# Three graph layers' edge loops: sums ahead of weights, features ahead of scaling, four product buffers

## The chip, the cores and the metric

The kernel runs on one core of a Trainium2 chip. Times are device microseconds of one execution. Engine names in the profile: PE is TensorE (PEld its weight loads), DVE is VectorE, ACT is ScalarE, POOL is GpSimd, SP is SyncE.

## The reference

The input is a graph of 6250 nodes (160 numbers each: 64 scalars and 32 vectors of three) and 100000 edges. Four layers run one after the other, each followed by a residual and a layer norm. The change is in layers 1 to 3. Each of them does this for every edge (layer 3 is shown; layer 1 has relu and no `e0`, layer 2 has no cross product and also counts edges):

```python
hid = silu(edge_scalars @ fc_w1 * _inv(R))
w = hid @ fc_w2 * _inv(FC_HID)
w1, w2, w3, w4, w5 = split(w, [64, 128, 160, 192], axis=-1)
es = h_s[edge_src];  ev = h_v[edge_src]
m_s1 = w1 * es * e0
m_s2 = w4 * einsum('eci,ei->ec', ev, e1) * _inv(3)
m_v1 = (w2 * es)[:, :, None] * e1[:, None, :]
m_v2 = w3[:, :, None] * ev * e0[:, :, None]
m_v3 = w5[:, :, None] * cross(ev, e1[:, None, :]) * _inv(2)
agg = segment_sum(concatenate(m_s1, m_s2, m_v1, m_v2, m_v3), edge_dst)
```

## The kernel before

Layer 0 has an edge loop of its own. Layers 1 to 3 share one function, `edge_loop(L)`, which the change edits. Edges lie sorted by destination block of 128 nodes. A step takes 256 edges (two groups `g` of 128) that all belong to one block, and each layer has 440 steps, four to an iteration of a hardware loop (`u` is 0 to 3). Below, step k is the k-th of the 440.

In each step of a layer the engines do this, joined by semaphores alone:

- SyncE loads the edges' records (`rec`, L840) and features (`efr`, L841) into one of four slots, after product k-4 is done.
- GpSimd gathers 2 times 128 node rows (L911) from HBM into `gatx`, after the record has landed.
- TensorE turns the features (`transposed`, L975), makes the hidden layer (`hidden`, L979) and the weights (`weights`, L985, 448 columns, into one of two banks `pW`), and adds up the products of one block with a one-hot matrix (`sums`, L993, twice 480 columns, 385 in layer 2, into one of two banks `pS`).
- ScalarE copies the turned features out of PSUM (`features`, L924), applies the activation (`activated`, L929), multiplies part of the weights by `e0` in place (`scaled`, L935, not in layer 1), and writes six blocks of the product (`axes`, L945, six instructions).
- VectorE makes the rest of the product (`product`, L1041 to L1070, in layer 2 to L1067) in one of two halves of `tp`, makes the one-hot matrix (L1056), and in the middle of it adds a finished sum to the block's row in SBUF (`keep`, L1081).

The order within an engine's step is written out by hand. TensorE's step k is: weights of step k+2, first half of the sums of k, transpose of k+3, second half of the sums of k, hidden layer of k+3. ScalarE's step k is: axes of k, scaling of k+1, features of k+2, activation of k+2. VectorE's product k has the keep of k-2 in it.

The waits that matter: `weights(k+2)` waits for the activation of k+2 and for product k (it frees the bank `pW`). `sums(k)` waits for product k, axes k and the keep of k-2 (bank `pS`). `hidden(k+3)` waits for the copy of the features of k+3. `features(k+2)` waits for the transpose of k+2. The product k waits for its gather, for `summed` of k-2 (half of `tp`) and for `w_done` of k, which is the scaling in layers 2 and 3 and the weights themselves in layer 1.

Of the kernel before, what the change touches and what calls it, by code (L numbers as in the profile page):

```python
# [12 lines left out]
G = 2  # L13
# [7 lines left out]
RH, TPW = 10, 544  # L21
# [43 lines left out]
def build(nc, ins, out, N, E, CH):  # L65
    fp32, i32 = mybir.dt.float32, mybir.dt.int32
    ALU, ACT, AX = mybir.AluOpType, mybir.ActivationFunctionType, mybir.AxisListType
# [6 lines left out]
    with ctx:  # L74
# [26 lines left out]
        def mark(name, total):  # L101
            if name not in known:
                known[name] = Mark(sem(name))
            known[name].base += known[name].total
            known[name].total = total
            return known[name]
# [48 lines left out]
        gat = sb("gat", [P, 4, G, F])  # L155
# [688 lines left out]
        def edge_loop(L):  # L844
# [13 lines left out]
            tp_ready = sig4("tp_ready", 1, NP)  # L858
            summed = sig4("summed", 1, NP)
            kept = sig4("kept", 1, NP)  # L860
            zeroed = mark("sums_zeroed", 2 + (L.n == 2))
            TW, VS = L.width, L.vs
            fc1, fc2 = W[f"fc1_{L.n}"], W[f"fc2_{L.n}"]
            EW = G * L.efw
            pE, pH, ramp = BK[0][:, 0:128], BK[0][:, 128:256], BK[1][:, 0:P]
            pW, pS = [BK[2], BK[3]], [BK[4], BK[5]]
            w_done = w_ready if L.y0 is None else w_scaled
            NM = 3 if L.cross else 1

            def w_of(u):  # L870
                return pW[u % 2][:, 0:448].rearrange("p (g f) -> p g f", g=G)

            def after(i, u, k):
                return (i, u + k) if u + k < 4 else (i + 1, u + k - 4)

            def last(u, k):
                return u + k < 4

            with nc.Block() as block:
# [19 lines left out]
                @block.gpsimd  # L899
                def _(po):  # L900
                    if L.n == 2:
                        nc.gpsimd.memset(tp[:, :, :, 64 + 384:64 + 385], 1.0).then_inc(zeroed.h, 1)

                    def gather(i, u):
                        po.wait_ge(rec_in[u].h, rec_in[u].at(i * 32 + 32))
                        po.sem_inc(pool_tick, 1)

                        po.wait_ge(tp_ready.h, tp_ready.free(i, u, 4))
                        po.sem_inc(pool_tick, 1)
                        for g in range(G):  # L910
                            nc.gpsimd.indirect_dma_start(  # L911
                                out=gatx[:, u, g, 0:L.row], out_offset=None, in_=tables[L.n][:, :],
                                in_offset=IOff(ap=rec[:, u, g, L.idx:L.idx + 1].bitcast(i32), axis=0))\
                                .then_inc(gat_in[u].h, 16)

                    with po.Fori(0, QP) as i:
                        for u in range(4):
                            gather(i, u)

                @block.scalar  # L920
                def _(ac):
                    def features(i, u):
                        ac.wait_ge(ef_t.h, ef_t.done(i, u))
                        nc.scalar.activation(efT[0:EW, u % 2, :], pE[0:EW, :], ACT.Copy).then_inc(ef_ready.h, 1)  # L924

                    def activated(i, u):
                        ac.wait_ge(hid.h, hid.done(i, u))
                        func, by = {1: (ACT.Relu, 1.0), 2: (ACT.Silu, 0.25), 3: (ACT.Silu, 0.125)}[L.n]
                        nc.scalar.activation(hT[:, u % 2, :], pH, func, scale=by).then_inc(hid_ready.h, 1)  # L929

                    def scaled(i, u):
                        ac.wait_ge(w_ready.h, w_ready.done(i, u))
                        for g in range(G):
                            c = slice(224 * g + 64, 224 * g + 160)
                            done = nc.scalar.activation(pW[u % 2][:, c], pW[u % 2][:, c], ACT.Copy,  # L935
                                                        scale=rec[:, u % 4, g, L.y0:L.y0 + 1])
                        done.then_inc(w_scaled.h, 1)

                    def axes(i, u):
                        ac.wait_ge(sv_ready.h, sv_ready.done(i, u))  # L940
                        t = tp[:, u % 2]
                        for g in range(G):
                            for k in range(3):
                                lo = 64 + 96 + VS * k
                                done = nc.scalar.activation(t[:, g, lo:lo + 64], t[:, g, 0:64], ACT.Copy,  # L945
                                                            scale=rec[:, u, g, L.y + k:L.y + k + 1])
                        done.then_inc(axes_done.h, 1)

                    def step(i, u, end=False):
                        axes(i, u)  # L950
                        if L.y0 is not None and (not end or last(u, 1)):
                            scaled(*after(i, u, 1))
                        if not end or last(u, 2):
                            features(*after(i, u, 2))
                            activated(*after(i, u, 2))

                    for u in range(2):
                        features(0, u)
                        activated(0, u)
                    if L.y0 is not None:  # L960
                        scaled(0, 0)
                    with ac.Fori(0, QP - 1) as i:
                        for u in range(4):
                            step(i, u)
                    for u in range(4):
                        step(QP - 1, u, True)

                @block.tensor
                def _(pe):
# [18 lines left out]
                    def sums(i, u, g):  # L988
                        if g == 0:
                            pe.wait_ge(tp_ready.h, tp_ready.done(i, u))  # L990
                            pe.wait_ge(axes_done.h, axes_done.done(i, u))
                            pe.wait_ge(kept.h, kept.free(i, u))
                        done = nc.tensor.matmul(pS[u % 2][:, 0:TW], oh[:, u, g, :], tp[:, u % 2, g, 64:64 + TW],  # L993
                                                start=g == 0, stop=g == G - 1)
                        if g == G - 1:
                            done.then_inc(summed.h, 1)

                    def step(i, u, end=False):
                        if not end or last(u, 2):
                            weights(*after(i, u, 2))  # L1000
                        sums(i, u, 0)
                        if not end or last(u, 3):
                            transposed(*after(i, u, 3))
                        sums(i, u, 1)
                        if not end or last(u, 3):
                            hidden(*after(i, u, 3))
# [13 lines left out]
                def _(ve):  # L1020
# [6 lines left out]
                        return bass.AP(tensor=a.tensor, offset=a.offset, ap=[a.ap[0]] + dims)  # L1027

                    def product(i, u, ahead):
                        t, w, row = tp[:, u % 2], w_of(u), gatx[:, u]  # L1030
                        tv = t[:, :, 160:160 + 3 * VS].rearrange("p g (i f) -> p g i f", i=3)
                        v = row[:, :, 64:160].rearrange("p g (k c) -> p g k c", k=3)

# [1 line left out]
                            return w[:, :, lo:lo + 32].unsqueeze(2).to_broadcast([P, G, 3, 32])  # L1035
                        ve.wait_ge(rec_in[u].h, rec_in[u].at(i * 32 + 32))
                        ve.wait_ge(gat_in[u].h, gat_in[u].at(i * 32 + 32))
                        ve.wait_ge(summed.h, summed.free(i, u))
                        ve.wait_ge(w_done.h, w_done.done(i, u))

                        nc.vector.tensor_tensor(t[:, :, 0:128].rearrange("p g (j c) -> p g j c", j=2),  # L1041
# [31 lines left out]
                    def block_of(i, u):  # L1073
                        return ve.value_load(L.blocks[0:1, bass.ds(i * 4 + u, 1)], min_val=0, max_val=NB - 1)

                    def keep(i, u, b):
                        ve.wait_ge(summed.h, summed.done(i, u))
                        row = acc[:, bass.ds(b, 1), :].rearrange("p o f -> p (o f)")

                        ve.wait_ge(kept.h, kept.free(i, u, 1))  # L1080
                        nc.vector.tensor_tensor(row, row, pS[u % 2][:, 0:TW], ALU.add).then_inc(kept.h, 1)  # L1081

                    ve.wait_ge(zeroed.h, zeroed.at(2 + (L.n == 2)))
                    for u in range(2):
                        product(0, u, None).then_inc(tp_ready.h, 1)
                    for u in range(2, 4):
                        product(0, u, (0, u - 2, block_of(0, u - 2))).then_inc(tp_ready.h, 1)
                    with ve.Fori(1, QP) as i:
                        for u in range(4):
                            back = (i - 1, u + 2) if u < 2 else (i, u - 2)  # L1090
                            product(i, u, (*back, block_of(*back))).then_inc(tp_ready.h, 1)
                    for u in range(2, 4):
                        keep(QP - 1, u, block_of(QP - 1, u))
                    ve.wait_ge(kept.h, kept.done(QP - 1, 3))

# [1045 lines left out]
```

## Time and profile before

| | us |
|---|---|
| median of 3 runs | 10883.89 (10879.81 to 10886.22) |
| the profiled execution's own time | 10889.87 |
| its span, first to last instruction | 10887.1 |
| edge loop of layer 1: first product to last | 5756.5 to 7258.5 |
| edge loop of layer 2 | 7567.9 to 9017.4 |
| edge loop of layer 3 | 9195.7 to 10698.6 |

Over the whole span TensorE is busy 81%, VectorE 80%, ScalarE 64% and GpSimd 59%. These shares are means over layer 0, three edge loops and the passes over nodes between them. The clock column of the windows is the granted TensorE clock as a share of full speed. In the timeline, a line's first number is the start in us from the span's start and the second the duration. "x2" merges two instructions, and brackets give the idle time before the instruction and what ended it.

### The profile page before, as it was taken

The page shows a single profiled execution, that of the slowest core. Times are in us where ns is not written, and L with a number is a line of the kernel's source. Part 1 is how long each engine was busy: PE and PEld are TensorE (multiplying, and loading weights), DVE is VectorE, ACT ScalarE, POOL GpSimd, SP SyncE. Part 2 cuts the span into 40 slices and gives each one's busy share as a digit, 9 for nine tenths or more (in the row PEclk, how much of TensorE's full clock was granted, in tenths as well). Part 3 has the DMA queues.
Part 4 walks back from the last instruction along what each step waited for, and adds up shares of the span by engine and source line. Part 5 has one row for each costly group of instructions (what it writes and reads, how often), then busy time and mean ns, then how long its engine had stood idle before and what let it go on. Part 6 is the DMA issues. An engine that isn't in the chain of part 4 may idle for free. (4 is left out here: it accounts for less than half of the span.)

```text
span 10887.1 us, 242413 instructions
## 1 busy us (share of the span) xinstructions
PE 8864.7 (81%) x46500; PEld 6212.8 (57%) x46501; DVE 8658.5 (80%) x31135; ACT 6961.3 (64%) x26255; POOL 6465.1 (59%) x9502
## 2 busy tenths in 40 slices
PE   3570069999999999999997888887888887888887
PEld 1250058888888888888884444445444445444445
DVE  6850069999999999999978999974666666999995
ACT  0020058888888888888875666644777775777774
POOL 0577777777777777777525555531555551555551
PEclk9965589999999999999999999985999998999996
DMA  7433322222222212221123444441333333444443
GB/s 292 44 82 73 71 42 37 36 37 36 37 36 37 36 35 37 36 36 34 20 43 84 90 89 89 89 67 36 58 58 58 58 57 66 90 90 90 90 89 58
DMA packets 1798441, 691.91 MB, mean 64 GB/s; under 512 B 1586190, under 2 KB 1677258, under 8 KB 1798346
## 3 DMA queue, kind: packets, MB, share of 16 engines
q0 software_dynamic: 219136, 411.56, 15.6%
q1 hardware_dynamic: 1572154, 275.26, 15.1%
q10 hardware_dynamic: 7056, 4.02, 0.1%
q8 instruction: 36, 0.59, 0.0%
q14 instruction: 59, 0.48, 0.0%
HBM read 514.24 MB, written 171.77 MB: 63 GB/s over the span
## 5 line engine op out<-in xcount | busy, mean ns | idle before, releaser
L911 POOL DMA_INDIRECT shared<-table,rec x2640 | 2564.6, 971 | 2236.0 <-DMA efr<-rec_dst 786.9
L993 PE MATMUL bank<-tp,oh 128*128 128x480 f32 (+1 forms) x5280 | 2352.4, 541 | 7.2 <-DVE tp L1070 4.2
L945 ACT ACTIVATE tp<-tp,rec 128x64 f32<-128x64 f32 x7920 | 2031.2, 335 | 239.3 <-DVE tp L1041 174.8
L985 PE MATMUL bank<-w_fc,hT 128*128 128x448 f32 x2640 | 1346.2, 592 | 589.2 <-ACT hT L929 573.0
L993 PEld LDWEIGHTS bank<-tp,oh 128*128 128x128 f32 x5280 | 902.0, 191 | 831.9 <-issue 819.4
L782 POOL DMA_INDIRECT rec_dst<-ACC x784 | 811.6, 1035 | 529.7 <-issue 497.3
L1041 DVE TENSOR_TENSOR tp<-bank,shared 128x256 f32<-128x256 f32 x1320 | 560.6, 425 | 653.9 <-PE bank L993 516.6
L1630 ACT ACTIVATE shared<-bank 128x512 f32<-128x512 f32 x1760 | 942.9, 586 | 122.1 <-PE bank L1705 119.3
L1594 POOL DMA_INDIRECT gat<-table,rec x880 | 889.5, 1011 | 220.5 <-issue 202.6
L929 ACT ACTIVATE hT<-bank 128x128 f32<-128x128 f32 x1320 | 366.5, 278 | 989.2 <-PE bank L979 964.3
L1581 POOL DMA_INDIRECT rec_src<-ACC x784 | 841.6, 1074 | 208.0 <-issue 185.4
L1705 PE MATMUL bank<-ident,tp 128*128 128x128 f32 x7040 | 933.2, 276 | 3.0 <-ACT tp L813 2.0
L985 PEld LDWEIGHTS bank<-w_fc,hT 128*128 128x128 f32 x2640 | 394.3, 188 | 835.6 <-DVE tp L1070 549.0
L979 PEld LDWEIGHTS bank<-efT,w_fc 128*128 128x128 f32 (+1 forms) x2640 | 457.7, 187 | 689.8 <-ACT efT L924 613.0
L1705 PEld LDWEIGHTS bank<-ident,tp 128*128 128x128 f32 x7040 | 830.6, 147 | 3.8 <-ACT tp L813 2.3
L1081 DVE TENSOR_TENSOR ACC<-ACC,bank 128x480 f32 (+1 forms) x1320 | 813.8, 616 | 4.2 <-PE bank L993 4.1
L1048 DVE TENSOR_TENSOR shared<-shared,rec 128x288 f32<-128x288 f32 x1760 | 722.4, 452 | 0.0
L1714 PE MATMUL bank<-w_vvlin,shared 128*128 128x32 f32 x5280 | 711.3, 272 | 0.0
L1659 ACT ACTIVATE shared<-shared,a 128x128 f32<-128x128 f32 x1760 | 562.4, 390 | 212.9 <-DVE a L1946 212.9
L1728 PEld LDWEIGHTS bank<-w_val,shared 128*128 128x128 f32 x5280 | 681.3, 192 | 0.0
L813 ACT ACTIVATE tp<-t_sv,rec 128x64 f32<-128x64 f32 x2640 | 674.1, 342 | 3.5 <-DVE t_sv L1845 3.5
L813 ACT ACTIVATE tp<-vsv,rec 128x64 f32<-128x64 f32 x2640 | 674.6, 339 | 0.0
(249 smaller groups left out, 21496.4 us busy)
## 6 DMA issues: line engine op xcount, KB each, us to landing
shared<-table,rec POOLq DMA_INDIRECT x2640
rec_dst<-tp SPq DMA_DIRECT2D x44, 900.0 KB, 23.6
ACC<-in_attrs SPq DMA_DIRECT2D x56, 623.0 KB, 5.1
rec_src<-tp SPq DMA_DIRECT2D x44, 730.0 KB, 19.8
efr<-rec_src SPq DMA_DIRECT2D x440, 64.0 KB
efr<-rec_dst SPq DMA_DIRECT2D x440, 64.0 KB
ACC<-in_attrs SPq DMA_DIRECT2D x196, 130.0 KB
rec<-rec_dst SPq DMA_DIRECT2D x1320, 10.0 KB
```

The source lines that it names most:

```text
L782: nc.gpsimd.indirect_dma_start(out=rec_dst[:, :], out_offset=IOff(ap=stage_i[:, u, c, 0:1], axis=0), in_=stage[:, u, c, 1:RD + 1], in_offs ...
L813: last = nc.scalar.activation(t[:, g, lo:lo + 64], s[:, g, :], ACT.Copy, scale=rec[:, u % 4, g, L.y + k:L.y + k + 1])
L911: nc.gpsimd.indirect_dma_start(out=gatx[:, u, g, 0:L.row], out_offset=None, in_=tables[L.n][:, :], in_offset=IOff(ap=rec[:, u, g, L.idx:L. ...
L945: done = nc.scalar.activation(t[:, g, lo:lo + 64], t[:, g, 0:64], ACT.Copy, scale=rec[:, u, g, L.y + k:L.y + k + 1])
L985: nc.tensor.matmul(pW[u % 2][:, 0:448], hT[:, u % 2, :], fc2[:, :], start=True, stop=True)\
L993: done = nc.tensor.matmul(pS[u % 2][:, 0:TW], oh[:, u, g, :], tp[:, u % 2, g, 64:64 + TW], start=g == 0, stop=g == G - 1)
L1048: done = nc.vector.tensor_tensor(vy[:, g], ranges(row[:, g, 64:65], [[32, 3], [32, 3], [1, 32]]), ranges(rec[:, u, g, L.y:L.y + 1], [[2, 3 ...
L1081: nc.vector.tensor_tensor(row, row, pS[u % 2][:, 0:TW], ALU.add).then_inc(kept.h, 1)
L1581: nc.gpsimd.indirect_dma_start(out=rec_src[:, :], out_offset=IOff(ap=srow_i[:, h, c, RS:RS + 1], axis=0), in_=srow[:, h, c, 0:RS], in_offs ...
L1594: nc.gpsimd.indirect_dma_start(out=gat[:, s4, g, :], out_offset=None, in_=tables[0][:, :], in_offset=IOff(ap=rec[:, s4, g, 1:2].bitcast(i3 ...
L1630: nc.scalar.activation(into[:, g, :], pT[g][:, :], ACT.Copy).then_inc(copied_.h, 1)
L1705: last = nc.tensor.transpose(pT[g][:, 128 * k:128 * k + 128], tp[:, slot, g, lo:lo + 128], ident[:, :])
```

## The change

In the edge loops of layers 1 to 3 the first half of the sums of step k is issued before the weights of k+2. ScalarE copies the features of k+2 before it scales the weights of k+1. There are four product buffers instead of two (the halves of `tp`, and two in the tiles `gat` and `shared`, which are free in these loops), and four sum banks instead of two. The keep in product k is now that of k-3. In layer 2 the constant column of ones is set in four buffers instead of two.

```diff
-            zeroed = mark("sums_zeroed", 2 + (L.n == 2))
+            zeroed = mark("sums_zeroed", 2 + 4 * (L.n == 2))
+            products = [tp[:, 0], tp[:, 1], gat.rearrange("p u g f -> p (u g f)")[:, 0:G * TPW].rearrange(
+                "p (g f) -> p g f", g=G), shared[:, 3136:3136 + G * TPW].rearrange("p (g f) -> p g f", g=G)]
-            pW, pS = [BK[2], BK[3]], [BK[4], BK[5]]
+            pW, pS = [BK[2], BK[3]], BK[4:8]
...
-                        nc.gpsimd.memset(tp[:, :, :, 64 + 384:64 + 385], 1.0).then_inc(zeroed.h, 1)
+                        for t in products:
+                            nc.gpsimd.memset(t[:, :, 64 + 384:64 + 385], 1.0).then_inc(zeroed.h, 1)
...
                     def step(i, u, end=False):
                         axes(i, u)
+                        if not end or last(u, 2):
+                            features(*after(i, u, 2))
                         if L.y0 is not None and (not end or last(u, 1)):
                             scaled(*after(i, u, 1))
                         if not end or last(u, 2):
-                            features(*after(i, u, 2))
                             activated(*after(i, u, 2))
...
-                            pe.wait_ge(kept.h, kept.free(i, u))
-                        done = nc.tensor.matmul(pS[u % 2][:, 0:TW], oh[:, u, g, :], tp[:, u % 2, g, 64:64 + TW],
+                            pe.wait_ge(kept.h, kept.free(i, u, 4))
+                        done = nc.tensor.matmul(pS[u][:, 0:TW], oh[:, u, g, :], products[u][:, g, 64:64 + TW],
...
                     def step(i, u, end=False):
+                        sums(i, u, 0)
                         if not end or last(u, 2):
                             weights(*after(i, u, 2))
-                        sums(i, u, 0)
...
-                        ve.wait_ge(summed.h, summed.free(i, u))
+                        ve.wait_ge(summed.h, summed.free(i, u, 4))
...
-                        nc.vector.tensor_tensor(row, row, pS[u % 2][:, 0:TW], ALU.add).then_inc(kept.h, 1)
+                        nc.vector.tensor_tensor(row, row, pS[u][:, 0:TW], ALU.add).then_inc(kept.h, 1)
...
-                            back = (i - 1, u + 2) if u < 2 else (i, u - 2)
+                            back = (i - 1, u + 1) if u < 3 else (i, 0)
```

## Rows read from the trace of the kernel before

**Rows 1.** Windows, each engine's busy time: steady stretches of layers 1, 2, 3.

```profile
core 0: us, PE busy (x) PEld busy (x) DVE busy (x) ACT busy (x) POOL busy (x), PEclk, DMA share, GB/s
...
5800.00:7150.00 1350.00, 1172.95 (x3572) 593.25 (x3570) 1286.86 (x3968) 830.45 (x3173) 786.10 (x794) 1.00 0.40 89
...
7600.00:8900.00 1300.00, 1124.26 (x3573) 543.32 (x3573) 857.79 (x2778) 953.07 (x3969) 749.67 (x794) 1.00 0.32 58
...
9250.00:10600.00 1350.00, 1174.27 (x3571) 592.62 (x3570) 1290.94 (x3967) 989.34 (x3967) 778.46 (x794) 1.00 0.41 90
```

**Rows 2.** Waits of TensorE and VectorE, layer 1, 5800 to 7150.

```profile
PE bank L985 <- ACT hT L929: 171.7, 387, 0.4
...
DVE tp L1041 <- DMA shared<-table,rec: 6.3, 13, 0.9
```

**Rows 3.** Waits of TensorE and VectorE, layer 2, 7600 to 8900.

```profile
PE bank L985 <- ACT hT L929: 175.3, 395, 0.4
...
DVE tp L1041 <- PE bank L993: 442.2, 397, 1.2
```

**Rows 4.** Waits of VectorE near the end of layer 2's loop, 8930 to 9020.

```profile
DVE tp L1041 <- DMA shared<-table,rec: 36.1, 24, 2.9
```

**Rows 5.** Timeline of one step of layer 1.

```profile
6305.57 0.42 DVE L1041 TENSOR_TENSOR tp<-bank,shared 128x256 f32<-128x256 f32 x1
...
6305.74 1.01 PE L985 MATMUL bank<-w_fc,hT 128*128 128x448 f32 x2 [0.45 <-DVE tp L1070]
...
6306.59 0.97 PE L993 MATMUL bank<-tp,oh 128*128 128x480 f32 x2
...
6307.40 0.27 PE L975 MATMUL bank<-ident,efr 128*128 128x128 f32 x1
...
6307.51 0.97 PE L993 MATMUL bank<-tp,oh 128*128 128x480 f32 x2
...
6308.31 0.38 PE L979 MATMUL bank<-efT,w_fc 128*128 128x128 f32 x2
...
6308.73 0.28 ACT L929 ACTIVATE hT<-bank 128x128 f32<-128x128 f32 x1 [0.75 <-PE bank L979]
6308.75 0.42 DVE L1041 TENSOR_TENSOR tp<-bank,shared 128x256 f32<-128x256 f32 x1
...
6309.14 1.01 PE L985 MATMUL bank<-w_fc,hT 128*128 128x448 f32 x2 [0.44 <-ACT hT L929]
```

**Rows 6.** Timeline of VectorE, layer 1, across a turn of the hardware loop.

```profile
6325.93 0.42 DVE L1041 TENSOR_TENSOR tp<-bank,shared 128x256 f32<-128x256 f32 x1
6329.47 0.42 DVE L1041 TENSOR_TENSOR tp<-bank,shared 128x256 f32<-128x256 f32 x1 [0.28 <-issue]
```

**Rows 7.** Timeline of the first three products of layer 2.

```profile
7567.87 0.42 DVE L1041 TENSOR_TENSOR tp<-bank,shared 128x256 f32<-128x256 f32 x1
...
7568.33 1.54 ACT L945 ACTIVATE tp<-tp,rec 128x64 f32<-128x64 f32 x6 [11.73 <-DVE tp L1041]
...
7569.78 0.51 ACT L935 ACTIVATE bank<-bank,rec 128x96 f32<-128x96 f32 x2
...
7570.42 0.43 DVE L1041 TENSOR_TENSOR tp<-bank,shared 128x256 f32<-128x256 f32 x1 [0.85 <-ACT bank L935]
...
7576.43 0.42 DVE L1041 TENSOR_TENSOR tp<-bank,shared 128x256 f32<-128x256 f32 x1 [4.31 <-PE bank L993]
```

**Rows 8.** Timeline of ScalarE in one steady step of layer 2.

```profile
8103.08 0.27 ACT L924 ACTIVATE efT<-bank 32x128 f32<-32x128 f32 x1
...
8104.15 0.28 ACT L929 ACTIVATE hT<-bank 128x128 f32<-128x128 f32 x1 [0.80 <-PE bank L979]
...
8104.32 1.53 ACT L945 ACTIVATE tp<-tp,rec 128x64 f32<-128x64 f32 x6
```

**Rows 9.** Timeline of GpSimd's gathers in layer 1.

```profile
6313.31 0.94 POOL L911 DMA_INDIRECT shared<-table,rec  x1 [2.14 <-issue]
```

**Rows 10.** Groups by line, shapes apart: gathers and longest two-input products, layer 1.

```profile
L911 POOL DMA_INDIRECT shared<-table,rec x794 | 786.9, 991 | 565.3 <-DMA efr<-rec_src 268.9 <-issue 156.5 <-DVE tp L1070 139.9
...
L1048 DVE TENSOR_TENSOR shared<-shared,rec 128x288 f32<-128x288 f32 x793 | 325.3, 452 | 0.0
```

**Rows 11.** Groups by line, shapes apart: gathers, layer 2.

```profile
L911 POOL DMA_INDIRECT shared<-table,rec x794 | 750.5, 945 | 550.0 <-DMA efr<-rec_dst 232.0 <-issue 182.6 <-DVE tp L1067 135.4
```

More of the change, by code:

```diff
@@ L940, in axes @@
                         ac.wait_ge(sv_ready.h, sv_ready.done(i, u))
-                        t = tp[:, u % 2]
+                        t = products[u]
                         for g in range(G):
@@ L1029, in product @@
                     def product(i, u, ahead):
-                        t, w, row = tp[:, u % 2], w_of(u), gatx[:, u]
+                        t, w, row = products[u], w_of(u), gatx[:, u]
                         tv = t[:, :, 160:160 + 3 * VS].rearrange("p g (i f) -> p g i f", i=3)
@@ L1080, in keep @@
                         ve.wait_ge(kept.h, kept.free(i, u, 1))
-                        nc.vector.tensor_tensor(row, row, pS[u % 2][:, 0:TW], ALU.add).then_inc(kept.h, 1)
-                    ve.wait_ge(zeroed.h, zeroed.at(2 + (L.n == 2)))
-                    for u in range(2):
+                        nc.vector.tensor_tensor(row, row, pS[u][:, 0:TW], ALU.add).then_inc(kept.h, 1)
+                    ve.wait_ge(zeroed.h, zeroed.at(2 + 4 * (L.n == 2)))
+                    for u in range(3):
                         product(0, u, None).then_inc(tp_ready.h, 1)
-                    for u in range(2, 4):
-                        product(0, u, (0, u - 2, block_of(0, u - 2))).then_inc(tp_ready.h, 1)
+                    product(0, 3, (0, 0, block_of(0, 0))).then_inc(tp_ready.h, 1)
                     with ve.Fori(1, QP) as i:
                         for u in range(4):
-                            back = (i - 1, u + 2) if u < 2 else (i, u - 2)
+                            back = (i - 1, u + 1) if u < 3 else (i, 0)
                             product(i, u, (*back, block_of(*back))).then_inc(tp_ready.h, 1)
-                    for u in range(2, 4):
+                    for u in range(1, 4):
                         keep(QP - 1, u, block_of(QP - 1, u))
```

## The prediction

> **What bounds the kernel now.** I read first the chain that ended last. It follows only the pass over nodes at the very end, so the loops have to be judged by their own stretches. The windows [rows 1] come next. Between the fills and the tails each loop is regular: two gathers to a step, so 794 gathers are 397 steps, and a step takes 1350/397 = 3.40 us in layers 1 and 3 and 1300/397 = 3.27 us in layer 2. VectorE is busy 1286.86/1350 = 95% in layer 1 and as much in layer 3. It looks like the bound there, yet in layer 2 it is busy 66%, ScalarE 73%, TensorE 86%, and nothing is full.
>
> The waits say what sets the pace. In both kinds of layer TensorE waits in nearly every step for the activation before it issues the weights: 387 times in 397 steps in layer 1 [rows 2], 395 times in layer 2 [rows 3]. In layer 2 VectorE stands 1.1 us in each step (442.2 us, 397 times) until a sum is complete [rows 3].
>
> One step in the timeline [rows 5] shows the circle. The weights start at 6305.74, first sums 6306.59, transpose 6307.40, second sums 6307.51, hidden layer 6308.31 (0.38 long), activation on ScalarE 6308.73 to 6309.01, and only then the next weights at 6309.14. That is 3.40 us from weights to weights. All of it is one chain: TensorE issues in order, and for some 0.44 us of each step it has nothing that it may do, although the next sums are nearly ready. VectorE's own interval in the same place is shorter, 6308.75 - 6305.57 = 3.18 us. So layers 1 and 3 are paced by TensorE's order, with VectorE close behind.
>
> **The change part by part.**
>
> *Sums ahead of weights.* The first sums of the next step need product and axes, not the activation. They fill the 0.44 us, and the activation has their 0.8 us to arrive in. No instruction is added on TensorE. Its own step becomes 6308.31 - 6305.74 = 2.57 us plus the hidden layer, which lasts 0.38 us by its record: at most 2.95 us [rows 5]. This is under VectorE's 3.18, so in layers 1 and 3 the pace goes to VectorE. What is late next is the loop's turn on VectorE. Every fourth interval is longer there, 6329.47 - 6325.93 = 3.54 us [rows 6], with 0.28 us in which nothing but its own instruction stream holds it. The mean is (3 x 3.18 + 3.54)/4 = 3.27 us. The gain is 3.40 - 3.27 = 0.13 us a step. The bounds are 0 (something else keeps 3.40) and 0.22 (the turn hides).
>
> *How many steps gain.* At the end of each loop VectorE waits for gathers step after step: 24 times in 90 us [rows 4]. Those steps are paced by DMA and gain nothing. With some 8 steps of filling, 440 - 24 - 8 = 408 steps gain. That is 0.13 x 408 = 53 us in each of layers 1 and 3.
>
> *Gathers.* In layer 1 VectorE waits 13 times for a gather, 6.3 us in all [rows 2]. TensorE's slower pace hides this today, since the stretch as a whole still runs at 3.40. Once VectorE paces, every such wait counts. A gather's lead spans three steps and shrinks by 3 x 0.13 = 0.4 us, so 6.3 + 13 x 0.4 = 11.5 us is the upper price and 0 the lower. I take 10 us a layer. GpSimd sometimes stands 2.14 us where 0.3 us is usual [rows 9]; I count these among the 13.
>
> *Features ahead of scaling, layers 2 and 3.* In layer 2 the circle of TensorE also passes through ScalarE. The activation comes at 8104.15, which is 0.80 us after the end of the features' copy (8103.08 + 0.27), and only then come the axes [rows 8]. With scaling (0.51 us) between copy and activation this idle time is filled. The price is that scaling stands later. The next product waits for it, and its axes for the product. That circle can be read off the start of layer 2, where nothing else holds VectorE [rows 7]: product 7567.87, axes 7568.33 (0.46 later), scaling 7569.78 (1.45), next product 7570.42 (0.64), which is 2.55 us a step. The copy now lies inside it. On ScalarE it takes between 0.17 us (the distance from an activation to the next start, 8104.32 - 8104.15) and its full 0.27 us [rows 8]. That gives 2.72 to 2.82 us. From the copy's start to the next axes the way through the activation is 0.27 + 0.80 + 0.17 = 1.24 us and the way through scaling and product at least 0.17 + 0.64 + 0.46 = 1.27 us, so the activation just hides. TensorE's busy time is 1124.26/397 = 2.83 us a step [rows 1]. This counts the overlap of records' ends, as in layer 1, where 1172.95/397 = 2.95 us meets the 2.95 above. The loop's turn adds 0 to (3.54 - 3.18)/4 = 0.09 us to the mean. The bounds are 2.72 and 2.91 us, and I take 2.85. The gain is 3.275 - 2.85 = 0.425 us a step, 408 steps, 173 us. The lead of the gathers shrinks by 3 x 0.425 = 1.3 us. Layer 2 has no wait for a gather in its steady stretch now [rows 3], so I take 5 us off for the rare 2.14 us stands.
>
> In layer 3 the same circle of 2.8 us stays below 3.27, so scaling is hidden by VectorE. If that cover were gone, it would cost the 0.2 to 0.3 us of the copy in each step.
>
> *Four buffers and banks.* They remove VectorE's wait for the sums of k-2. In the new order these sums are complete about 0.85 (first sums) + 0.85 (weights) + 0.11 (transpose) + 0.97 (second sums) = 2.8 us after product k-2 ends [rows 5], and product k-1 takes 3.18 us in layer 1. So the order alone would already free VectorE there, with 0.4 us to spare, and I give the buffers no gain of their own; the upper bound of their worth is that same 0.13 us a step. Keep k-3 is the same instruction. One keep moves from the middle to the loop's end and runs while TensorE still adds up: 0. The two more memsets in layer 2 stand under the fill: 0.
>
> *Sum.* 2 x (53 - 10) + (173 - 5) = 254 us. The profiled execution took 10889.87 us, 6 us over the median of 10883.89, so it would be 10636 and the median 10630 us.
>
> **The rivals.**
>
> *TensorE is already full.* If its busy time in layer 2 is real occupancy and the hidden layer's latency is not hidden, the step there is 3.0 instead of 2.85 us. For it speaks 86% busy; against it, that the gap of 0.44 us is idle in the records. The time is 254 - 0.15 x 408 = 193 us less: 10691 us.
>
> *VectorE's layers do not move.* The 95% busy in layers 1 and 3 [rows 1] is the whole truth and gathers eat the rest. Only layer 2 gains: 168 us, 10716 us. The interval of 3.18 us speaks against it.
>
> *The gathers are held up by VectorE.* GpSimd needs 0.95 + 0.30 us for a gather, 2.5 us a step. A gather lasts 991 ns on average while VectorE is 95% busy [rows 10] and 945 ns at 66% [rows 11]. If a fuller VectorE held each one back by a whole product of 0.45 us [rows 10], two would take 3.4 us a step, and no loop would be faster than today. It decides from 3.27/2 - 1.25 = 0.38 us a gather. The 46 ns between those two rows speak against it. I give it 10884 us at worst, 10800 as its middle. The Trainium skill, in SBUF — State Buffer, section Who interferes with whom, says that a VectorE instruction with two SBUF inputs and a GpSimd instruction that reads SBUF contend for a shared port pair under an exclusive lock, and the loser blocks for the whole instruction. By that rule the hold-up could reach the full product; this trace shows 46 ns on the mean.
>
> *Slower.* TensorE's granted clock is 1.00 in all three stretches [rows 1]. At the start of layer 2, at a lower clock, one product follows the other after 7576.43 - 7570.42 = 6.01 us [rows 7], 3.16 us more than 2.85. If the denser issue made the clock fall within the loops, 254/3.16 = 80 steps of the 1224 at that pace would undo the gain, and 120 of them give 11009 us. Against it: the clock holds at 1.00 with TensorE 87% busy, and the gaps now go.
>
> **How the numbers follow.** Forecast 0.65 (10580 to 10680), TensorE full 0.12, VectorE's layers unmoved 0.11, gathers held up 0.04, slower 0.03, and 0.05 for more than forecast (turn hidden, 2.72 us in layer 2: down to 10510). The range 10565 to 10745 holds the first three cases and leaves out about 0.12. What a measurement can tell from no change is about 0.2%, 22 us. Faster by more 0.94, same 0.03, slower 0.03.
>
> **What would show it.** In the profile after, the weights should have no wait for the activation. VectorE's wait at L1041 for sums should be gone, and in layer 2 replaced by a short one for the scaling. The intervals of L1041 should be 3.18 and 3.54 us in layers 1 and 3 and near 2.8 us in layer 2. VectorE should be about 99% busy in layers 1 and 3 and 76% in layer 2. A wait of the transpose for records, of L1041 for gathers in every step, or a clock below 1.00 in the loops would prove it wrong.

## The result and the profile after

| | before | after |
|---|---|---|
| median, us | 10882.53 (4 runs) | 10612.53 (4 runs, 10607.52 to 10614.03) |
| ratio | | 0.9747, 95% interval 0.9735 to 0.9758 |
| the profiled execution's own time | 10889.87 | 10607.52 |
| edge loop of layer 1, first product to last | 1502.0 | 1454.4 |
| layer 2 | 1449.5 | 1263.9 |
| layer 3 | 1502.9 | 1455.5 |

The kernel became 270 us faster; 254 were forecast. The loops give 47.6 + 185.6 + 47.4 = 280.6 us between the two profiled executions, whose times differ by 282. Outside the loops next to nothing moved.

The windows of the changed kernel, steady stretches of layers 1, 2 and 3, in the columns of [rows 1]:

```profile
5800.00:7130.00 1330.00, 1197.98 (x3634) 603.25 (x3632) 1290.83 (x4036) 833.73 (x3231) 785.93 (x807) 1.00 0.42 92
7550.00:8680.00 1130.00, 1110.88 (x3589) 544.22 (x3588) 860.41 (x2790) 956.24 (x3986) 756.12 (x798) 1.00 0.38 67
9010.00:10330.00 1320.00, 1187.74 (x3609) 599.10 (x3608) 1282.73 (x4008) 1001.64 (x4008) 782.58 (x801) 1.00 0.42 93
```

With two gathers to a step, a step takes 1330/403.5 = 3.30 us in layer 1, 1130/399 = 2.83 us in layer 2 and 3.30 us in layer 3, where it took 3.40, 3.27 and 3.40 [rows 1]. VectorE is busy 97% in layer 1 and 76% in layer 2. In layer 2 TensorE is busy 98%: that is the number to keep in mind. The clock stays at 1.00.

Waits of TensorE in layer 1, 5800 to 7130:

```profile
PE bank L997 <- DVE tp L1074: 82.0, 199, 0.8
PE bank L997 <- DVE gat L1074: 23.3, 99, 0.7
PE bank L997 <- DVE shared L1074: 23.0, 100, 0.7
```

The 387 waits for the activation [rows 2] are gone, and TensorE now waits in nearly every step for VectorE's last product instruction (L1074). The two engines have changed places. Waits of VectorE in layer 2, 7550 to 8680, beside the 442.2 us for sums [rows 3]:

```profile
DVE tp L1045 <- ACT bank L938: 122.8, 188, 0.8
DVE gat L1045 <- ACT bank L938: 58.9, 92, 0.8
DVE shared L1045 <- ACT bank L938: 56.3, 96, 0.6
DVE tp L1045 <- DMA shared<-table,rec: 17.4, 12, 2.0
DVE gat L1045 <- DMA shared<-table,rec: 9.8, 7, 1.7
DVE shared L1045 <- DMA shared<-table,rec: 4.4, 4, 1.3
```

It waits for the scaling (L938), 376 times, and 23 times for a gather. The timeline of VectorE's first product instruction in layer 1, across a turn of the loop, answers to [rows 5] and [rows 6]:

```profile
6316.63 0.42 DVE L1045 TENSOR_TENSOR gat<-bank,shared 128x256 f32<-128x256 f32 x1
...
6319.80 0.42 DVE L1045 TENSOR_TENSOR shared<-bank,shared 128x256 f32<-128x256 f32 x1
...
6323.34 0.42 DVE L1045 TENSOR_TENSOR tp<-bank,shared 128x256 f32<-128x256 f32 x1 [0.28 <-issue]
```

The intervals are 3.17 us, and 3.54 us at the turn. One step of layer 2 on TensorE and ScalarE:

```profile
8104.23 0.91 PE L997 MATMUL bank<-tp,oh 128*128 128x385 f32 x2
...
8104.34 0.28 ACT L932 ACTIVATE hT<-bank 128x128 f32<-128x128 f32 x1 [0.39 <-PE bank L983]
...
8104.51 1.53 ACT L948 ACTIVATE gat<-gat,rec 128x64 f32<-128x64 f32 x6
...
8104.98 0.92 PE L989 MATMUL bank<-w_fc,hT 128*128 128x448 f32 x2
...
8105.73 0.27 PE L979 MATMUL bank<-ident,efr 128*32 128x128 f32 x1
...
8105.84 0.81 PE L997 MATMUL bank<-tp,oh 128*128 128x385 f32 x2
8106.59 0.48 PE L983 MATMUL bank<-efT,w_fc 32*128 32x128 f32 x2
...
8107.00 0.92 PE L997 MATMUL bank<-gat,oh 128*128 128x385 f32 x2
```

First sums, weights, transpose, second sums, hidden layer and the next first sums stand end to end, with no wait in brackets: 2.77 us. ScalarE's activations come 2.76 us apart (8104.34, and 8107.10 in the next step). So the pace can be that of TensorE's work or that of a circle through ScalarE. Which of them holds is a question for the chip.

### The profile page after: what moved, and what is told of

Same layout as the page of the kernel before. It is cut to its first block and busy times, and to the rows that moved or that the text cites. A ratio compares the mean times of both kernels' runs of the same rounds, so it can differ in the third digit from the quotient of the medians.

```text
span 10605.0 us, 244487 instructions
## 1 busy us (share of the span) xinstructions
PE 8843.7 (83%) x46500; PEld 6209.7 (59%) x46501; DVE 8615.3 (81%) x31135; ACT 6948.2 (66%) x26255; POOL 6456.4 (61%) x9505
## 5 line engine op out<-in xcount | busy, mean ns | idle before, releaser
L997 PE MATMUL bank<-tp,oh 128*128 128x480 f32 (+1 forms) x2640 | 1281.1, 567 | 198.6 <-DVE tp L1074 184.9
L948 ACT ACTIVATE tp<-tp,rec 128x64 f32<-128x64 f32 x3960 | 1017.4, 335 | 335.4 <-DVE tp L1045 322.6
L989 PE MATMUL bank<-w_fc,hT 128*128 128x448 f32 x2640 | 1216.4, 543 | 3.1 <-ACT hT L932 3.1
L989 PEld LDWEIGHTS bank<-w_fc,hT 128*128 128x128 f32 x2640 | 502.0, 190 | 496.9 <-issue 417.7
L997 PE MATMUL bank<-shared,oh 128*128 128x480 f32 (+1 forms) x1320 | 637.8, 565 | 58.2 <-DVE shared L1074 56.5
L997 PE MATMUL bank<-gat,oh 128*128 128x480 f32 (+1 forms) x1320 | 637.7, 565 | 54.8 <-DVE gat L1074 51.3
L997 PEld LDWEIGHTS bank<-tp,oh 128*128 128x128 f32 x2640 | 397.6, 190 | 478.3 <-issue 280.6
```

The costliest lines, as they stand in the source:

```text
L989: nc.tensor.matmul(pW[u % 2][:, 0:448], hT[:, u % 2, :], fc2[:, :], start=True, stop=True)\
L997: done = nc.tensor.matmul(pS[u][:, 0:TW], oh[:, u, g, :], products[u][:, g, 64:64 + TW], start=g == 0, stop=g == G - 1)
```

## The experiments

Ratios are to the kernel before, run on the same chip. Mean steps are the windows' length over half their gathers.

**Which part carries the gain.** Four kernels.

`e1_buffers` has four buffers and banks, and both orders as before:

```diff
                     def step(i, u, end=False):
-                        sums(i, u, 0)
                         if not end or last(u, 2):
                             weights(*after(i, u, 2))
+                        sums(i, u, 0)
```

and ScalarE's step again as axes, scaling, features, activation.

> Four buffers and banks alone, both orders as before. If TensorE's order sets the pace (the theory of the prediction), the step stays at 3.40 us in layers 1 and 3 and 3.27 us in layer 2, VectorE's wait at its first product instruction only changes its releaser, and the time is that of before, 10883 us within 20 us. If VectorE was held by the two buffers (rival), the step falls towards 3.27 us in layers 1 and 3 and the time is below 10800 us.

Measured: 10881.01 us, ratio 0.9995 (0.9986 to 1.0005). Waits of TensorE and VectorE in its layer 2, 7600 to 8900:

```profile
PE bank L988 <- ACT hT L932: 175.9, 397, 0.4
...
DVE tp L1044 <- ACT bank L938: 243.2, 198, 1.4
```

TensorE waits for the activation 397 times as before [rows 3]. VectorE's wait has a new releaser, the scaling, and the pace is the same (1350/397 = 3.40 us in layer 1, 1300/397 = 3.27 in layer 2). The buffers alone are worth nothing.

`e2_orders` is the opposite: both new orders in the kernel before, two buffers and two banks.

> Both new orders, but two buffers and banks as before. By the prediction the sums of k-2 are complete 2.8 us after product k-2 ends and VectorE needs 3.18 us for product k-1 in layers 1 and 3, so all steps run as in the changed kernel (3.29, 2.84, 3.29 us on the mean) and the time is 10613 us within 20 us. If the buffers let the gain through (rival), layer 2, where product k-1 takes only 2.2 us, steps at over 2.95 us and the time is over 10660 us.

Measured: 10622.45 us, ratio 0.9756 (0.974 to 0.9773). A step takes 1330/404 = 3.29 us in layer 1 and 1130/397.5 = 2.84 us in layer 2. The interval overlaps that of the changed kernel, so what the buffers add in company, if anything, is not resolved: the two medians are 10 us apart.

`e3_scaling_first` is the changed kernel with one edit undone:

```diff
                         axes(i, u)
-                        if not end or last(u, 2):
-                            features(*after(i, u, 2))
                         if L.y0 is not None and (not end or last(u, 1)):
                             scaled(*after(i, u, 1))
                         if not end or last(u, 2):
+                            features(*after(i, u, 2))
                             activated(*after(i, u, 2))
```

> The changed kernel with ScalarE's order of before (scaling, then the features' copy). Theory: ScalarE's own circle then has the 0.80 us from copy to activation idle in it: axes 1.45 + scaling 0.51 + copy 0.27 + 0.80 + 0.17 = 3.20 us. Layer 2 steps at 3.20 us instead of 2.84 us, layer 3 nearly unchanged (3.20 against 3.29 us of VectorE), layer 1 unchanged (no scaling). Time 10613 + 0.36 x 408 = 10760 us. Rival: ScalarE's order is idle detail and TensorE's order gives all; then 10613 us.

Measured: 10685.44 us, ratio 0.9816 (0.980 to 0.9833), so this edit is worth 73 us of the 270, not the 147 expected. Layer 2 steps at 1180/392 = 3.01 us, layers 1 and 3 are unchanged. ScalarE in its layer 2:

```profile
8103.60 0.25 ACT L927 ACTIVATE efT<-bank 32x128 f32<-32x128 f32 x1
...
8104.43 0.28 ACT L932 ACTIVATE hT<-bank 128x128 f32<-128x128 f32 x1 [0.57 <-PE bank L982]
...
8106.73 0.25 ACT L927 ACTIVATE efT<-bank 32x128 f32<-32x128 f32 x1
```

From the end of the copy to the activation it is 0.58 us here, not the 0.80 of [rows 8]. In the kernel before, the second sums still occupied TensorE when the copy was done, and 0.2 us of the 0.80 were that. With 0.58 the expected sum becomes 1.45 + 0.51 + 0.27 + 0.58 + 0.17 = 2.98 us, near the 3.01 measured.

`e4_weights_first` is the changed kernel with TensorE's order of before (the diff of `e1_buffers`, alone).

> The changed kernel with TensorE's order of before (weights, then the first sums). Theory: TensorE's circle through the activation comes back, 3.40 us in layers 1 and 3 and 3.27 us in layer 2, in spite of four buffers and ScalarE's new order: 10883 us within 20 us. Rival: one of the other two parts carries part of the gain; then the time lies between 10613 and 10860 us.

Measured: 10881.81 us, ratio 0.9998 (0.9988 to 1.0007). TensorE's waits in its layer 2, 7600 to 8900:

```profile
PE bank L989 <- ACT hT L932: 175.2, 395, 0.4
```

The 395 waits for the activation are here again. Without the sums ahead of the weights, buffers and ScalarE's order together are worth nothing. With them, ScalarE's order gives 73 us on top of some 200.

**What holds layer 2 at 2.77 us.** Theory A is the prediction's circle (axes, copy, scaling, product), theory B that TensorE is full. Two kernels leave out work in layer 2 alone. `x1_half_scaling`:

```diff
-                        for g in range(G):
+                        for g in range(1 if L.n == 2 else 0, G):
                             c = slice(224 * g + 64, 224 * g + 160)
```

> The changed kernel; in layer 2 only the second of the two scaling instructions is left, so the weights of one group of edges stay unscaled. Layer 2 now steps at 2.77 us (2.84 on the mean). Theory A, the prediction's: the circle through axes, copy, scaling and product sets it. Then it falls by the instruction's 0.22 us, to about 2.60. Theory B: TensorE is full there (its rows stand back to back in 2.77 us). Then the step stays at 2.77 us within 0.03.

`x2_half_sums`:

```diff
-                        done = nc.tensor.matmul(pS[u][:, 0:TW], oh[:, u, g, :], products[u][:, g, 64:64 + TW],
+                        w = 193 if L.n == 2 and g == 1 else TW
+                        done = nc.tensor.matmul(pS[u][:, 0:w], oh[:, u, g, :], products[u][:, g, 64:64 + w],
```

> The changed kernel; in layer 2 the second half of the sums covers 193 columns instead of 385, so half of the columns miss one group's edges. This takes 0.32 us of work off TensorE and nothing off the others. Theory B (TensorE full): the step falls from 2.77 us until the next circle holds it; from the rows of e3 that is axes 1.53, copy to scaling to product 0.71, product to axes 0.46, so 2.65 to 2.70 us. Theory A (circle through scaling): it stays at 2.77 us.

`x3_both_halved` has both edits.

> Both cuts at once, layer 2 only. Under theory B with A's circle as the next in line the step falls below either cut alone, to what is left on ScalarE: axes 1.53, and 0.83 + 0.17 us from the copy through the hidden layer and the activation back to the axes, 2.53 us. If it is no lower than in the run with the sums halved, scaling is in no circle that holds.

These three ran on a second chip, on which the kernel before takes 11278 us. They took 11366, 11310 and 11332 us in one run each, with mean steps in layer 2 of 3.7 to 3.8 us. Stalls and a lower granted clock outweigh every circle there (below), and the three are inconclusive. The first two were run again on a third chip, where the kernel before takes 10891 us, beside the changed kernel.

> The changed kernel again, beside the next three. The last four kernels ran on a chip on which the kernel before takes 11278 us instead of 10883: gathers there land late over and over. If this call falls on a chip like the first, the ratio is 0.975 again and a step of layer 2 is 2.84 us on the mean. If it falls on one like the second: a gather's lead is 0.4 us shorter in layers 1 and 3 and 1.3 us shorter in layer 2 than before the change, so I expect the gain to be lost there, a ratio between 0.995 and 1.01, with mean steps of about 3.55, 3.7 and 3.6 us.

> As the run with one of two scaling instructions in layer 2 (the weights of one group of edges stay unscaled), to be read where gathers are not late. Circle through scaling (theory A): layer 2 steps at about 2.60 us. TensorE full (theory B): 2.77 us within 0.03, 2.84 on the mean or a little less at the loop's turn.

> As the run with 193 instead of 385 columns in the second sums of layer 2 (half of the columns miss one group's edges), to be read where gathers are not late. Theory B (TensorE full): the step falls from 2.77 to 2.65 or 2.70 us. Theory A (circle through scaling): it stays at 2.77 us.

Measured: the changed kernel 10610.96 us, ratio 0.9743 (0.973 to 0.9756), the first result once more. `y1_half_scaling` 10617.64 us and `y2_half_sums` 10589.96 us in one run each; the argument rests on their steps, not on these times. With half of the scaling gone, layer 2 steps at 1130/397 = 2.85 us, no faster. Its timeline on ScalarE:

```profile
8103.56 0.25 ACT L927 ACTIVATE efT<-bank 32x128 f32<-32x128 f32 x1
8103.72 0.28 ACT L938 ACTIVATE bank<-bank,rec 128x96 f32<-128x96 f32 x1
...
8104.57 0.28 ACT L932 ACTIVATE hT<-bank 128x128 f32<-128x128 f32 x1 [0.57 <-PE bank L983]
...
8107.34 0.28 ACT L932 ACTIVATE hT<-bank 128x128 f32<-128x128 f32 x1 [0.61 <-PE bank L983]
```

The time taken off the scaling comes back as a longer wait for the hidden layer, 0.57 to 0.61 instead of 0.39 us, and from activation to activation it is 2.77 us as before. Theory A falls. Its circle is real, though, and shows by itself in single steps behind a late gather, when TensorE is ahead. First the changed kernel, then `y1_half_scaling`:

```profile
8121.57 0.42 DVE L1045 TENSOR_TENSOR tp<-bank,shared 128x256 f32<-128x256 f32 x1 [0.68 <-ACT bank L938]
...
8124.17 0.42 DVE L1045 TENSOR_TENSOR tp<-bank,shared 128x256 f32<-128x256 f32 x1 [0.44 <-ACT bank L938]
```

```profile
8101.66 0.42 DVE L1045 TENSOR_TENSOR gat<-bank,shared 128x256 f32<-128x256 f32 x1 [1.06 <-DMA shared<-table,rec]
...
8104.03 0.42 DVE L1045 TENSOR_TENSOR shared<-bank,shared 128x256 f32<-128x256 f32 x1 [0.21 <-ACT bank L938]
```

The circle takes 2.60 us whole (product to axes 0.46, to copy 1.45, to scaling 0.16, to product 0.53) and 2.37 us with half of the scaling, both shorter than 2.77.

With the second sums halved, TensorE and ScalarE in layer 2:

```profile
8100.97 0.92 PE L998 MATMUL bank<-gat,oh 128*128 128x385 f32 x2
...
8102.58 0.49 PE L998 MATMUL bank<-gat,oh 128*128 128x193 f32 x2
8102.85 0.25 ACT L927 ACTIVATE efT<-bank 32x128 f32<-32x128 f32 x1
...
8103.15 0.29 PEld L983 LDWEIGHTS bank<-efT,w_fc 32*128 32x128 f32 x2 [0.38 <-ACT efT L927]
8103.15 0.48 PE L983 MATMUL bank<-efT,w_fc 32*128 32x128 f32 x2
...
8103.56 0.91 PE L998 MATMUL bank<-shared,oh 128*128 128x385 f32 x2
```

The step shown takes 2.59 us, 0.18 less. By their records the second sums became 0.32 us shorter (0.49 for 0.81), but from their start to the hidden layer it is only 0.18 less (0.57 for 0.75): the hidden layer's weights now wait for the features' copy, which ends at 8103.10. Less work on TensorE made the step shorter, so theory B stands, and the step falls until the circle of theory A holds it, at its 2.60 us. The mean falls only from 2.83 to 1130/405 = 2.79 us. Two of the four steps of an iteration run at 2.60 us, the other two at 2.84 and 2.79 us. In the first of them VectorE's product starts 0.28 us after the scaling's end (8103.51 to 8103.79) where 0.03 is usual. In the second TensorE's first sums start 0.66 us after the hidden layer (8106.00 to 8106.66) where 0.41 is usual. These look like the loop's turns of VectorE and of TensorE; no run took either away by itself in this layer.

TensorE's turn is in the changed kernel too: from one hidden layer to the next it is 2.77 us, and once in four steps 2.94 us or a little more (8100.88 to 8103.82). Four steps without a late gather take 11.23 us in the median, 2.81 us a step.

**The loop's turn.** The changed kernel with the block's number read later, and nothing left out:

```diff
-                            keep(*ahead)
+                            keep(*ahead, block_of(*ahead))
...
-                            product(i, u, (*back, block_of(*back))).then_inc(tp_ready.h, 1)
+                            product(i, u, back).then_inc(tp_ready.h, 1)
```

> The changed kernel; VectorE reads the block's number just before the keep in the middle of the product, not ahead of the product. Nothing is left out. Theory: in layers 1 and 3 the 3.53 us interval at the loop's turn is VectorE's instruction stream (branch, then reading the number, before the next product may start); with the reading under the product's long instructions the turn falls to 3.2 to 3.3 us, 0.06 to 0.08 us a step, 50 to 65 us in both layers, and the time is about 10555 us. Rival: the reading holds up the keep instead and each step gets up to 0.3 us longer: 10613 to 10850 us.

> The late reading of the block's number again. Its turn of the loop took 3.18 to 3.21 us on the second chip instead of 3.53, but the mean was all waits for gathers. On a chip like the first: 408/4 x 0.35 us in each of layers 1 and 3, 70 us less than the changed kernel, at most the waits for gathers that this uncovers (some 10 us): about 10550 us, ratio 0.970. On a chip like the second: no different from the changed kernel beside it, within 0.3%.

Measured on the second chip (`x4_late_block`): 11327.85 us, ratio 1.0048 (1.0032 to 1.0064). On the third (`y4_late_block`): 10565.09 us, ratio 0.9699 (0.9686 to 0.9713), 46 us less than the changed kernel beside it, not 70. It is the fastest version here. The timeline of VectorE's first product instruction in its layer 1, across a turn:

```profile
6301.38 0.41 DVE L1045 TENSOR_TENSOR shared<-bank,shared 128x256 f32<-128x256 f32 x1
...
6304.55 0.41 DVE L1045 TENSOR_TENSOR tp<-bank,shared 128x256 f32<-128x256 f32 x1
...
6307.74 0.42 DVE L1045 TENSOR_TENSOR tp<-bank,shared 128x256 f32<-128x256 f32 x1
```

VectorE's longest waits in its layer 2:

```profile
DVE ACC L1085 <- issue: 75.6, 384, 0.3
DVE tp L1045 <- DMA shared<-table,rec: 39.8, 39, 2.3
```

The turn lies between the product into `shared` and that into `tp`, and its interval is 3.17 us; the next is 3.19. Layer 1 falls from 3.30 to 1300/403 = 3.23 us and layer 3 from 3.30 to 1320/408.5 = 3.23. But in layer 2, where VectorE's instructions are fewer, the reading is no longer hidden and holds the keep by 0.2 us in each step (75.6 us, 384 times), and the mean step rises from 2.83 to 1130/394.5 = 2.86. Its waits for gathers grew too, to 39.8 + 10.6 + 4.8 us from 31.6, so how much of the 0.03 us is the reading is not shown. The theory is right in layers 1 and 3, and what the rival named is to be seen in layer 2. Reading late in layers 1 and 3 alone was not tried.

**The second chip.** The expectation of `y0_changed_again` blamed gathers that land late. The profile of `x4_late_block` says otherwise. Its waits of VectorE in layer 2, 7800 to 9200, have 29 waits for gathers, 26 us in 1400. Around 7960 us its timeline shows this:

```profile
7960.06 0.95 POOL L914 DMA_INDIRECT shared<-table,rec  x1 [0.30 <-issue]
7962.69 0.50 SPq L840 DMA_DIRECT2D rec<-rec_dst  x1
7962.70 0.28 ACT L932 ACTIVATE hT<-bank 128x128 f32<-128x128 f32 x1 [4.67 <-remote]
7962.74 0.56 DVE L1085 TENSOR_TENSOR ACC<-ACC,bank 128x385 f32 x1 [3.11 <-issue]
...
7963.03 0.30 PEld L989 LDWEIGHTS bank<-w_fc,hT 128*128 128x128 f32 x2 [4.39 <-ACT hT L932]
```

ScalarE, VectorE and SyncE begin again within 0.05 us of each other. ScalarE and VectorE stood 3 to 5 us before, and their brackets name no other engine. The hidden layer, which the activation at 7962.70 reads, had ended at 7958.16. So at least ScalarE did not stand for its data. What stops the engines is open.

The granted clock is lower there as well, 0.91 in layer 2:

```profile
7800.00:9200.00 1400.00, 1197.17 (x3432) 556.24 (x3433) 858.91 (x2672) 914.42 (x3815) 721.80 (x763) 0.91 0.29 52
```

TensorE is busy 1197.17/381.5 = 3.14 us in a step, against 1110.88/399 = 2.78 in the changed kernel at 1.00. In the three kernels that leave out work it was 0.90, 0.86 and 0.82. Whether the stops bring the clock down, or something else does both, was not separated. The profile of the kernel before on that chip was not taken, and the changed kernel itself did not run there: that its gain is lost there too is likely from `x4_late_block`, and not shown.

## Why the prediction was right

**The bound.** TensorE's order through the activation paced all three layers. Shown by `e1_buffers` and `e4_weights_first`: whatever else is changed, 395 to 397 waits and 3.40 and 3.27 us remain.

**Layers 1 and 3.** The forecast was 3.27 us a step and 43 us a layer, the measurement 3.30 us and 47.6 and 47.4 us. VectorE paces them with 3.17 and, at the turn, 3.54 us. That the turn is its own instruction stream is shown by `y4_late_block`, where it vanishes. Gathers cost 7.8 + 2.3 + 0.7 us in layer 1, 14 waits, against 10 us taken. VectorE is busy 97%, not the 99% that was expected.

**How many steps gain.** The last 24 steps are still paced by gathers, as the prediction had it: they take 87.7 us after 87.8 in layer 1, 85.2 after 88.0 in layer 2, and 87.3 after 87.8 in layer 3. The first 8, which it counted as gaining nothing, gained 2.3, 4.1 and 2.1 us.

**Layer 2.** The forecast was 2.85 us and 168 us, the measurement 2.83 us and 185.6 us. The size came out right from the wrong circle, and that was luck: two errors met. The prediction took axes, copy, scaling and product to set the pace (2.72 to 2.82 us) and set TensorE's busy time of 2.83 us aside as overlap of records' ends.

The first error is the circle. `y1_half_scaling` shows that it does not hold; `y2_half_sums` shows TensorE does, at 2.77 us between turns. The rival "TensorE is already full" had the mechanism, with 3.0 us a wrong price. The work could nearly have been laid end to end from the kernel before, one step of its layer 2:

```profile
8104.55 1.01 PE L985 MATMUL bank<-w_fc,hT 128*128 128x448 f32 x2 [0.44 <-ACT hT L929]
...
8106.90 0.48 PE L979 MATMUL bank<-efT,w_fc 32*128 32x128 f32 x2
```

That is 2.35 us from the weights to the hidden layer, and at most 0.48 for the hidden layer: 2.83 us.

The second error is the circle's length. Alone it takes 2.60 us. Scaling to product is 0.53 us in a steady step, not the 0.64 read at the layer's start [rows 7], and the copy adds 0.16. With 2.60 to 2.69 us in the place of 2.85, the prediction's own sum would give about 10530 to 10565 us, an estimate and 50 to 80 us too low.

The wait for scaling that the prediction asked to see is there (376 times) and proves nothing, since scaling is what the product waits for last in any circle that passes ScalarE.

**Gathers in layer 2** were priced at 5 us. There are 23 waits of 17.4 + 9.8 + 4.4 = 31.6 us. Not all of it is lost, since VectorE would else have waited for the scaling and the next steps catch up (the 2.60 us above). From 2.81 us without them to 2.83 us on the mean they cost some 10 us in 399 steps, an estimate. The steps at 2.81 instead of 2.85 us made up for it.

**ScalarE's order.** The mechanism was right, the stall of 0.80 us was 0.58 once TensorE's order is changed. So the edit is worth 73 us and not most of layer 2: with TensorE's order and the buffers alone, layer 2 is at 3.01 us.

**Buffers.** No gain of their own, as said; in `e2_orders` the medians are 10 us apart, which the intervals do not resolve.

**Gathers held up by VectorE** did not come. A gather in layer 1 lasts 974 ns on the mean now, with VectorE 97% busy, against 991 before [rows 10]:

```profile
L914 POOL DMA_INDIRECT shared<-table,rec x807 | 785.9, 974 | 544.5 <-DMA efr<-rec_src 278.8 <-issue 196.8 <-DVE tp L1074 61.4
```

By the rule of the Trainium skill (SBUF — State Buffer, Who interferes with whom) a full block would have shown as up to 0.45 us; this trace has none of that size on the mean. The same section says that `tensor_tensor`, which these products are, was not seen to stall a DMA, and with that the trace agrees.

**Slower** did not come: the clock stayed at 1.00. Its price of 6.01 us a step was not the clock's alone. It was read while the layer fills, 4.31 us of it a wait for the first sums, with a granted clock of 0.58 (7570 to 7577).

## What to carry to other kernels

When an in-order engine waits in every step for a result that it ordered itself a moment ago (weights, then activation, then weights), put work that is already ready between the order and its use, before buying buffers. Four buffers without the order gave nothing; the orders without the buffers gave all but some 10 us. A wait at an instruction names what came last, not the circle that sets the pace: take a piece of work off each circle and see whether the step gets shorter or another wait longer. A forecast whose size comes true can still name the wrong circle. On an engine near 100%, look at the loop's turn too: where a register is read may be worth more than an instruction, and the same place can gain in one layer and not in another.

## What the runs showed of the hardware

VectorE's turn of a four-step loop cost 0.37 us of its stream (3.54 against 3.17 us) with the number read ahead of the product, and nothing with it read under long instructions (3.17 us at the turn, 3.19 us in the interval behind it). The Trainium skill (Advanced Engine Details and Errata, Control Flow Timing) gives 108 ns for compare and branch; on VectorE in layers 1 and 3 the branch by itself is hidden in these traces, and the reading was the cost. On TensorE in layer 2, which has no such reading, the turn is to be seen: 1.37 us from the second sums to the next first sums in one turn (8111.38 to 8112.75), where it is 1.16 us without a turn.

One chip of the three ran the kernel before 3.6% slower (11278 against 10886 and 10891 us). In the one profile read closely there, of `x4_late_block`, several engines stop at once and the granted clock is 0.91 in layer 2. There the fastest version elsewhere, 3% ahead, was 0.5% behind. A gain that comes from closing gaps may not be found on every chip.
